# Attention on one core: two units share the rows of a result, and the output projection becomes three products of high and low parts

## What is computed

```
x = x + tanh(g_xattn[0]) * L0_xattn(layernorm(x), ctx_2048, Wq, bq, Wk, bk, Wv, bv, Wo, bo)
# in L0_xattn, with 8 heads of 8 channels:
q, k, v = W @ input + b          # per batch, over 64 channels
q, k = rope(q), rope(k)
p_attn = softmax(q @ k.T / sqrt(8))
out = p_attn @ v                 # (heads, positions, 8) -> (64, positions)
return Wo @ out + bo
```

## Time and profile before

| | |
|---|---|
| median of 3 runs | 1477.27 us (1472.82 to 1483.8) |
| the profiled execution | 1483.34 us, its span 1481.4 us |
| attention | from 0 to about 495 us of the span |
| PE, PEld, DVE, ACT, POOL busy over the span | 91%, 70%, 62%, 52%, 46% |
| mean granted clock of PE over the span | 0.96 |

### The profile page before, as it was taken

How to read it: one execution, slowest core, us unless ns; L and a number is a source line. 1 busy time by engine, 2 the same in 40 slices (tenths; PEclk the granted TensorE clock), 3 DMA queues, 4 the chain that set the end, 5 groups by cost and what they waited for, 6 DMA issues and landing times. The chain is left out here.

```text
span 1481.4 us, 31918 instructions
## 1 busy us (share of the span) xinstructions
PE 1353.9 (91%) x10082; PEld 1029.7 (70%) x10083; DVE 920.5 (62%) x1685; ACT 765.3 (52%) x1461; POOL 682.0 (46%) x850
## 2 busy tenths in 40 slices
PE   4899999999999499998999999999956899999998
PEld 3555555555555277777877888888854787877887
DVE  7889999998995377656544333333334566655653
ACT  0577777777778433431333333333324666556642
POOL 7667677676671166342664423200045544454220
PEclk9999999999999699999999999999955999999999
DMA  3222222222220131113752333211160001111000
GB/s 100 91 83 72 83 85 73 80 82 79 80 66 23 49 125 47 44 57 102 234 180 79 94 92 96 67 50 53 43 208 29 27 28 33 43 39 34 15 15 29
DMA packets 88481, 107.61 MB, mean 73 GB/s; under 512 B 11280, under 2 KB 79248, under 8 KB 87760
## 3 DMA queue, kind: packets, MB, share of 16 engines
q1 hardware_dynamic: 78656, 74.57, 15.8%
q0 software_dynamic: 9744, 31.99, 6.7%
HBM read 54.10 MB, written 25.03 MB: 53 GB/s over the span
## 5 line engine op out<-in xcount | busy, mean ns | idle before, releaser
L468 ACT ACTIVATE e_t<-st_ps 128x512 f32<-128x512 f32 x512 | 278.5, 598 | 109.2 <-PE st_ps L556 103.5
L406 DVE TENSOR_REDUCE row_max<-s_ps 128x4 f32<-128x1024 f32 x256 | 311.9, 1220 | 30.0 <-PE s_ps L561 28.0
L556 PE MATMUL st_ps<-q_st,k_st 32*128 32x256 f32 x1024 | 158.2, 330 | 8.3 <-ACT e_t L468 3.6
L577 PE MATMUL o_ps<-e_t,v_st 128*32 128x256 f32 x2048 | 164.1, 392 | 0.6
L561 PE MATMUL s_ps<-k_st,q_st 32*128 32x256 f32 x1024 | 156.2, 339 | 5.1 <-DVE row_max L406 3.6
L556 PEld LDWEIGHTS st_ps<-q_st,k_st 32*128 32x128 f32 x1024 | 103.4, 184 | 60.0 <-issue 45.7
L1739 POOL DMA_INDIRECT gathered_tail<-sorted_results,result_at x64 | 70.2, 1097 | 154.0 <-POOLq L2230 135.7
L1976 DVE TENSOR_TENSOR h_all_tail<-silu_tail,u_ps_tail 128x512 f32<-128x512 f32 x64 | 43.9, 685 | 127.5 <-ACT silu_tail L1847 68.5
L1597 PE MATMUL y_ps_moe<-w_all_moe,xt_hi_moe 128*128 x568 | 114.6, 285 | 5.0 <-DVE xt_lo_moe L1415 5.0
L1421 DVE TENSOR_TENSOR h_all_moe<-silu_moe,u_ps_moe 128x512 f32<-128x512 f32 x71 | 48.8, 688 | 109.1 <-PE u_ps_moe L1575 109.1
L1099 ACT COPY y_sb_moe<-y_ps_moe 128x256 f32<-128x256 f32 x71 | 26.4, 372 | 165.9 <-PE y_ps_moe L1597 165.9
(11 more groups left out here) (337 smaller groups left out, 3700.6 us busy)
## 6 DMA issues: line engine op xcount, KB each, us to landing
k_st<-k_part SPq DMA_DIRECT2D x96, 128.0 KB
q_st<-q_part SPq DMA_DIRECT2D x96, 128.0 KB
stage_moe<-in_experts POOLq DMA_DIRECT2D x21, 512.0 KB
rows_in_moe<-sorted_rows SPq DMA_DIRECT2D x71, 128.0 KB
sorted_results<-y_sb_moe SPq DMA_DIRECT2D x71, 128.0 KB
c_in<-in_ctx SPq DMA_DIRECT2D x32, 128.0 KB
x_sb<-in_x SPq DMA_DIRECT2D x32, 128.0 KB
xn_moe<-in_ctx SPq DMA_DIRECT2D x8, 512.0 KB
```

The costliest lines, as they stand in the source:

```text
L406: nc.vector.tensor_reduce(out, s_ps[p % 2][:], AX_X, ALU.max).then_inc(s["max_taken"], 1)
L468: nc.scalar.activation(e_t[t % 4][:, b, :, :], st_ps[:, b, :, :], ACT.Exp, scale=float(DH) ** -0.5)\
L556: last = nc.tensor.matmul(out, w, moving, start=True, stop=True)
L577: last = nc.tensor.matmul(o_ps[32 * j:32 * j + 32, u % 2, :], v_st[r][:, half_, u * UH + j, :], e_t[(2 * u + j // 2) % 4][:, j % 2, half_, :],
```

## The change

Four things are edited, all in `attention` and in the layout of its weights.

1. `o_ps` and `o_sb` become half as wide. Of two units, the even one writes rows 0 to 8 of each block of 32 rows and the odd one rows 16 to 24, in the same columns. For that the weights of the odd unit start 16 columns earlier in `v_st`, where zeros stand, and both units accumulate in one group of four matmuls. The number of matmuls in line 577 stays.
2. `turn_out` has two transposes where it had four. DVE reads the result with a stride of 16 where it was 32.
3. The output projection is three matmuls of float32r parts, high x high, low x high, high x low, where it was one float32 product of `w_out` and `a_t`. The parts of `w_out` are made once (`split_out`, body n = -2) by POOL. The parts of `a_t` are made in each body by POOL (`split_result`), between `normalize` and the k parts. PE waits for them (`a_split`) ahead of the projection in p = 6.
4. The order of the channels in `w_out` and the value bias follows the new row order.

```diff
-        o_sb = [sb(f"o_sb{r}", [P, 2, D]) for r in range(2)]
+        o_sb = [sb(f"o_sb{r}", [P, D]) for r in range(2)]
-        o_ps = ps("o_ps", [P, 2, D])
+        o_ps = ps("o_ps", [P, D])
 # GpSimd
+            def split_out():
+                pool.wait_ge(more_consts_in, 3 * 16)
+                nc.gpsimd.tensor_copy(out_high[:], w_out[:]).then_inc(s["out_high_made"], 1)
+                pool.wait_ge(s["out_high_made"], 1)
+                nc.gpsimd.tensor_tensor(out_low[:], w_out[:], out_high[:].bitcast(F32), ALU.subtract)\
+                    .then_inc(s["out_low_made"], 1)
+            def split_result(tile):
+                pool.wait_ge(s["a_taken"], tile + 1)
+                wait_count(pool, s["y_projected"], tile)
+                wait_alone(pool)
+                nc.gpsimd.tensor_copy(a_high[:], a_t[:]).then_inc(s["a_high_made"], 1)
+                pool.wait_ge(s["a_high_made"], tile + 1)
+                nc.gpsimd.tensor_tensor(a_low[:], a_t[:], a_high[:].bitcast(F32), ALU.subtract).then_inc(s["a_split"], 1)
                 if isinstance(n, int) and n == -2:
                     clear_rest()
+                    split_out()
                 if there(n, c, 3):
                     normalize(n, 3)
+                if there(n, c, -2):
+                    split_result(n - 2)
 # ScalarE, p == 3
-                        wait_count(act, s["y_projected"], n - 2)
+                        wait_count(act, s["a_split"], n - 2)
                         nc.scalar.copy(a_t[:], misc[:, 0:D]).then_inc(s["a_taken"], 1)
 # TensorE
+                    values = v_st[r][:, half_, :, :].rearrange("p h d -> p (h d)")
                     for j in range(UH):
-                        last = nc.tensor.matmul(o_ps[32 * j:32 * j + 32, u % 2, :], v_st[r][:, half_, u * UH + j, :],
+                        at = 32 * (u * UH + j) - 16 * (u % 2)
+                        last = nc.tensor.matmul(o_ps[32 * j:32 * j + 32, :], values[:, at:at + 32],
                                                 e_t[(2 * u + j // 2) % 4][:, j % 2, half_, :],
-                                                start=(half_ == 0), stop=(half_ == 1))
+                                                start=(half_ == 0 and u % 2 == 0), stop=(half_ == 1 and u % 2 == 1))
             def turn_out(b):
-                for half_, u in ((h, u) for h in range(2) for u in range(2)):
-                    at = (2 * half_ + u) * P
-                    last = nc.tensor.transpose(misc[:, at:at + P], o_sb[b][:, u, half_ * P:(half_ + 1) * P],
-                                               ident[:])
+                for half_ in range(2):
+                    part_of = slice(half_ * P, (half_ + 1) * P)
+                    last = nc.tensor.transpose(misc[:, part_of], o_sb[b][:, part_of], ident[:])
                 last.then_inc(s["o_turned"], 1)
 # TensorE, p == 6
-                        nc.tensor.matmul(misc[:, 0:D], w_out[:], a_t[:], start=True, stop=True)\
-                            .then_inc(s["y_projected"], 1)
+                        pe.wait_ge(s["a_split"], n - 1)
+                        for k, (w, part_of) in enumerate(((out_high, a_high), (out_low, a_high), (out_high, a_low))):
+                            last = nc.tensor.matmul(misc[:, 0:D], w[:], part_of[:], start=(k == 0), stop=(k == 2))
+                        last.then_inc(s["y_projected"], 1)
```

More of the change, by code:

```diff
@@ L132, in attention @@
         a_t = sb("a_t", [P, D])
+        a_high = sb("a_high", [P, D], F32R)
+        a_low = sb("a_low", [P, D], F32R)
+        out_high = sb("out_high", [P, P], F32R)
+        out_low = sb("out_low", [P, P], F32R)
         y_sb = sb("y_sb", [P, D])
@@ L152, in attention @@
                  "v_projected v_stored scored max_taken m_high m_split m_turned m_taken "
-                 "st_scored exp_done pv_done o_taken o_turned rcp_ready o_normed a_turned a_taken "
+                 "st_scored exp_done pv_done o_taken o_turned rcp_ready o_normed a_turned a_taken a_high_made a_split out_high_made out_low_made "
                  "y_projected y_taken y_free").split()
@@ L408, in normalize_out @@
             def normalize_out(tile, b):
-                o = misc[:].rearrange("p (h r) -> p h r", r=32)
+                o = misc[:, 0:D].rearrange("p (h r) -> p h r", r=16)
                 k = 2 * tile + b
@@ L2248, in layouts @@
     plain, plain_batch = np.tile(np.arange(CH), 2), np.repeat(np.arange(2), CH)
+    paired = np.arange(CH).reshape(2, UH, DH).transpose(1, 0, 2).ravel()
     wq, wk, wv, wo = (a[f"L0_xattn_W{m}"].T for m in "qkvo")
@@ L2258, in layouts @@
                           per_batch(wv, plain, plain_batch)], 1),
-        "w_out": per_batch(wo, plain, plain_batch),
-        "bias": np.stack([bq[ch_of], bq[swap], bk[ch_of], bk[swap], bo[plain], bv[plain]], 1),
+        "w_out": per_batch(wo[paired], plain, plain_batch),
+        "bias": np.stack([bq[ch_of], bq[swap], bk[ch_of], bk[swap], bo[plain], bv[np.tile(paired, 2)]], 1),
         "rope": np.stack(rotary_tables(), 1),
```

## The result

The kernel after takes 1584.47 us (median of 4 runs, 1578.68 to 1589.26), the kernel before 1475.94 us in the same comparison. The ratio is 1.0711 with a 95% interval of 1.0672 to 1.0751. The sign and the mechanism are those of the prediction, the size is not: +108.5 us where +79 was forecast, outside the range of 1515 to 1575. One of the rivals, the clock staying low for longer, had been given 1585 us and a chance of 0.09.

What follows compares the result with a forecast made beforehand. PE was taken as the bound (busy 361.00 of 364 us), the late split on POOL making a loop that sets the period. Loop +48.3, clock +31 and ends -0.5 us on 1477.3 gave 1556 us, range 1515 to 1575.

Steps and rivals of the forecast that it cites:

- the clock staying low for longer: Rival on PE's clock in attention: each fall holds twice as long, 60 us in place of 31; 1585 us, chance 0.09.
- The new wait: PE's projection in p = 6 waits for POOL's late split: 7.76 us after `q_roped` ends, not 5.46; +2.30 us per body.
- The projection: Output projection on PE: three float32r matmuls take 0.56 us against 0.63 for two float32 instructions; -0.07 us per body.
- Half the copy, half the transposes: ACT's copy and PE's `turn_out(0)`, between p = 7's first score and `q_roped`'s end: 0.22 us saved each, -0.44 per body.
- Falls behind 23 of 27 pauses: PE's new pause of about 2.45 us lowers the granted clock in 6 of 7 cases, 23 of 27 bodies; +31 us.
- What a fall costs: Time lost on PE behind the pause, at half clock for 3.4 us: 1.35 us per fall, bounds 0 and 1.68.
- The rival with the clock up: Rival on PE's clock in attention: it stays up despite the pause, leaving only the longer loop; 1525 us, chance 0.20.
- The ends: Outside the 27 bodies: `split_out` +0.7 us, last body's uncovered split +1.3, savings in bodies 29 to 33 -2.5; together -0.5.

Runs made afterwards that it cites:

- e1: Kernel after with `split_result` moved on POOL from behind the normalization to ahead of it; 1464.3 us, ratio 0.992.
- e4: Kernel before plus the `split_result` pair on POOL, its parts read by no engine and PE not waiting for them; 1474.6 us, ratio 0.999.
- e5: Kernel before plus the `split_result` pair on POOL and PE's wait for it ahead of the old float32 projection; 1580.2 us, ratio 1.071.
- e2: Kernel before with the shared rows alone (half the copy, two transposes for four), float32 projection, no split on POOL; 1460.5 us, ratio 0.991.
- e7: Kernel after, pause kept, with 12 extra full-size matmuls in p = 7 ahead of the value projection; 1568.3 us, ratio 1.064.
- e9: Kernel after, pause kept, with 6 extra full-size matmuls in p = 7 ahead of the value projection; ratio 1.078 (1572.7 us on a faster chip).
- e8: Kernel after with 3 filling matmuls on constants ahead of PE's wait for the split; 1560.8 us, ratio 1.059.
- e3: Kernel after with 18 filling matmuls on constants ahead of PE's wait for the split; 1526.7 us, ratio 1.035.

## Why the prediction was right and wrong

The marks are those of the prediction: R is the end of `q_roped`, Y the output projection, S the first score behind it.

- **The new wait, +2.30 us per body.** Right, and shown by e1, e4 and e5. The projection came 7.76 us after R (207.00 less 199.24, the end of `q_roped` that released `q_bare` at 199.32), the predicted 7.76 to the hundredth, because it is a sum of POOL's instructions without a wait between them. The pause was 2.2 us and not 2.45: I had let the shorter `turn_out(0)` bring PE to it 0.22 us earlier, but PE then waits for the vector engine. In e2, too, the time from R to Y stays at 5.46 us. The row is of the kernel after:

```profile
202.78 0.38 PE L533 MATMUL misc<-k_input_high,w_high 128*128 128x256 f32 x1 [0.22 <-DVE a_sb L440]
```

- **The projection, -0.07.** From the first of three products to the next score are 0.51 us against 0.63: -0.12. Right in sign and of no weight.
- **Half the copy, half the transposes, -0.44 from S to R.** Right for the edit alone, wrong in the kernel after. In e2 a body is 0.43 us shorter, nearly all of it from S to R (7.48 us where it was 7.90). In the body of after shown above, S is at 207.51 and R at 215.36, 7.85 us: -0.05; in the two others without time at half clock it is 7.75. e5, which shares no rows, has 7.70 to 7.87 in such bodies. So with the pause in the loop sharing gains nothing there. What differs is on the vector engine. The same stretch of DVE (and in e2 the cast of POOL beside it) in two kernels, first after (S at 207.51) and then e2 (S at 201.84), whose `m_parts` and `a_sb` have the same code:

```profile
209.50 0.26 DVE L419 TENSOR_SCALAR m_parts<-row_max 128x32 fp32r<-128x32 f32 x1
209.79 0.67 DVE L421 SCALAR_TENSOR_TENSOR m_parts<-row_max,m_parts 128x32 fp32r<-128x32 f32 x1
210.38 1.21 DVE L430 TENSOR_REDUCE row_max<-s_ps 128x4 f32<-128x1024 f32 x1
...
211.79 0.29 DVE L440 TENSOR_TENSOR a_sb<-misc,o_rcp 128x128 f32<-128x128 f32 x1
...
212.23 0.27 PE L636 MATMUL misc<-ident,m_parts 128*64 128x128 f32 x1 [0.19 <-DVE a_sb L440]
```

```profile
203.72 0.18 DVE L416 TENSOR_SCALAR m_parts<-row_max 128x32 fp32r<-128x32 f32 x1
203.93 0.40 POOL L318 CAST k_part<-k_whole 128x256 fp32r<-128x256 f32 x1 [0.16 <-POOL k_whole L311]
203.94 0.43 DVE L418 SCALAR_TENSOR_TENSOR m_parts<-row_max,m_parts 128x32 fp32r<-128x32 f32 x1
204.30 1.21 DVE L427 TENSOR_REDUCE row_max<-s_ps 128x4 f32<-128x1024 f32 x1
...
205.71 0.29 DVE L437 TENSOR_TENSOR a_sb<-misc,o_rcp 128x128 f32<-128x128 f32 x1
...
206.18 0.30 PE L633 MATMUL misc<-ident,m_parts 128*64 128x128 f32 x1
```

The two `m_parts` hold up the row maximum by 0.88 us in the one and 0.58 in the other. `a_sb` comes 4.28 us after S and not 3.87, and PE, which in e2 goes on without idle time, waits for it. From S to the first matmul of the q projection are 6.06 us (213.57) against 5.77 (207.61). Over the 27 bodies the second `m_parts` instruction takes 307 ns on the mean in e2 and 476 in after, with the same 32 elements, and the first 182 and 377. What stands beside them differs: in e2 POOL has its cast of `k_part` there and then, from 204.41, a subtraction; in the kernel after POOL's block lies otherwise against S, and two instructions with two operands cover the pair:

```profile
208.99 0.73 POOL L320 TENSOR_TENSOR k_part<-k_whole,k_part 128x256 fp32r<-128x256 f32 x1
209.68 0.73 POOL L364 TENSOR_TENSOR x_sb<-x_sb,y_sb 128x256 f32 x1
```

The Trainium skill's page "SBUF — State Buffer", section "Who interferes with whom", has a rule for the second: a vector instruction with two SBUF inputs and a GpSimd instruction that reads SBUF exclude each other. The traces agree. Of the 324 such instructions in the 27 bodies of the twelve traces, the 91 that started while no GpSimd instruction ran took 0.19 us, the 93 that started inside a cast 0.27 to 0.43, and the 140 that started inside a GpSimd instruction with two operands 0.60 to 0.70. The first `m_parts` has one input from SBUF and slows too; that sentence of the page does not cover it. So what makes `m_parts` long is seen, but that this is what cost the loop its 0.3 us is argued: in e2 a second `m_parts` of 0.43 us makes a body no longer than one of 0.19 does, and no run took the contention away alone. The loop at full clock was 16.06 us and not 15.78: 54.9 us where I had 48.3.
- **Falls behind 23 of 27 pauses.** Right, 22.
- **What a fall costs, 1.35 us.** This is the step that failed, and it carries the miss. It measured 56.0 / 22 = 2.5 us, and the term 56 in place of 31. I had taken the length of a stretch, 3.4 us, from six falls in the stages of the experts and of the tail; in attention they last 8.2 us. The price per microsecond was fair (0.31 us lost for each at half clock, 0.4 in my sum). The sign of it was twice in the trace of before. From 44.0 to 50.4 us PE is busy for 5.63 of 6.40 us and still at half pace. (The trace has no record of the clock before 50.4 us, and the clock columns show 1.00 there; the pace is told by the durations, 0.41 us for a score where it is 0.27 at full clock.) And one stretch from 1074.4 to 1112.0 us, behind a pause of 11.5 us that I had left out of my count of pauses from 1.81 to 3.13 us, has 11.26 us of work without idle time in it, and stays at half clock. Its matmuls have 8 columns:

```profile
49.44 0.41 PE L556 MATMUL st_ps<-q_st,k_st 32*128 32x256 f32 x1
...
1074.40:1112.00 37.60, 23.19 (x98) 22.14 (x99) 13.66 (x43) 9.48 (x15) 17.13 (x20) 0.50 0.63 205
...
1083.66 11.26 PE L2167 MATMUL y_ps_tail<-attn,context_tail 128*128 128x8 f32 x52 [11.54 <-issue]
```

I had the longer stretches as a rival and gave them 0.09 for want of a reason why attention should differ. e5, e7 and e9 point to one: there is less full-size work behind the pause in attention. They do not prove it, and it need not be the only one.
- **The rival with the clock up.** Refuted in attention, by the kernel after at 2.1 us and by e8 at 1.6 us. It was also what the Trainium skill's page "TensorE: Matmul & The Clock Gate", section "Why this matters for your kernels", would have had; the trace disagrees.
- **The ends, -0.5 us.** They came to +2.1 us: 2.2 before the first of the 27 bodies and -0.1 behind the last. That the 2.2 come from `split_out` is not shown: e2, which has none, starts its first of these bodies at 73.3 us, before at 69.0 and after at 71.2.
- **The range.** Its upper end let every body fall at 1.68 us, which was a bound for one short stretch, not for the cost. The 1585 us of the rival should have been inside.

## What to carry to other kernels

A queue with idle time on average may have none where the new work is put: look for the one wait that holds its slack, and put the work on the side of it where its input is ready and its reader has not yet come. Work out from the list when the result will be there against when the in-order reader gets to it; here six places in a list decided between 0.8% faster and 7.1% slower. Where the change leaves a new pause of one or two microseconds on PE in every round of a loop, count the half clock behind it as a cost of its own, with a range that reaches to several times the shortest stretch seen, and test it by filling the pause.

## What the runs showed of the hardware

- The granted clock can stay at 0.50 for 12 us and more while PE is busy all of the time (224 to 236 us above). Up to 17.1 us were seen in the kernel after. They were shorter in the runs with more full-size work behind the pause: 8.2 us on the mean in the kernel after, 5.5 in e5, 4.7 in e9, 3.9 in e7.
- A pause that lowers the clock is not told by its length alone: pauses of 1.57 to 1.71 us did in attention (e8, 21 of 22), 1.74 to 1.79 did not in the tail, and 2.2 us did not in 20 bodies of e7.
- Filling idle time of PE with useless work can pay: 18 matmuls without use per body took 58 us off the time (e3).
- A small vector instruction with two inputs (`m_parts`, 32 elements) took 0.19 us alone and 0.60 to 0.70 when it started inside a two-operand GpSimd instruction of 0.73 us.
